# Moving the second FFN's row normalisation and quantisation into the attention batches of a two-layer kernel

## The reference

```python
x = x + _L1_xattn_ref(_layernorm(x), ctx_1024, ctx_1024, mask, Wq, bq, Wk, bk, Wv, bv, Wo, bo)
x = x + _L1_ffn_ref(_layernorm(x), gate_w, up_w, down_w, s_in, s_in_down)

def fake_quant_nvfp4(x, global_scale):       # blocks of 16 numbers
    amax = jnp.max(jnp.abs(xb), axis=-1, keepdims=True)
    sc8 = jnp.clip(amax / 6.0 * global_scale, 0.0, 448.0).astype(float8_e4m3fn).astype(float32)
    dq = sc8 / global_scale
    a = jnp.clip(jnp.abs(xb) / dq, 0.0, 6.0)
    return jnp.sign(xb) * nearest_of(0, 0.5, 1, 1.5, 2, 3, 4, 6)(a) * dq

def _L1_ffn_ref(x, ...):
    hidden = silu(fq(x) @ fq(gate_w).T) * (fq(x) @ fq(up_w).T)
    return fq(hidden) @ fq(down_w).T
```

## Time and profile before

| what | value |
|---|---|
| runs | 706.92 us median of three (706.83 to 707.96) |
| the profiled execution | 708.72 us, span 706.6 us |
| PE busy | 569.6 us (81% of the span) |
| DVE busy | 505.7 us (72%) |
| ACT busy | 377.0 us (53%) |
| POOL busy | 213.2 us (30%) |
| mean granted TensorE clock | 0.918 of full speed |
| chain that ended last | PE 42%, DVE 23%, ACT 13% of the span |

### The profile page before, as it was taken

One profiled execution on the slowest core, in us unless ns is written; L12 is line 12 of the kernel. 1 busy time (PEld: TensorE's weight loads), 2 busy tenths in 40 slices (PEclk: granted clock), 3 DMA queues, 4 the chain that ended last, 5 costly groups with the idle time before them and its releaser, 6 DMA issues.

```text
span 706.6 us, 14547 instructions
## 1 busy us (share of the span) xinstructions
PE 569.6 (81%) x4543; PEld 417.5 (59%) x4552; DVE 505.7 (72%) x1418; ACT 377.0 (53%) x717; POOL 213.2 (30%) x243
## 2 busy tenths in 40 slices
PE   5399999609999999976799999997535876687677
PEld 3188888509998898864466666664212453355345
DVE  6358887695655556573456666666769999999987
ACT  1324443113343333323666777778765878785674
POOL 5725774524665455552121443310000000000000
PEclk9789999959999999996899999999757999999999
DMA  8884443269466655607000000000000000000001
GB/s 317 271 221 132 129 150 119 71 217 387 148 220 200 204 180 179 207 28 241 1 2 0 0 0 0 0 1 2 4 1 0 31 15 16 31 30 16 16 30 60
DMA packets 35540, 68.49 MB, mean 97 GB/s; under 512 B 5581, under 2 KB 24542, under 8 KB 34464
## 3 DMA queue, kind: packets, MB, share of 16 engines
q1 hardware_dynamic: 28816, 52.37, 22.8%
q0 software_dynamic: 5520, 13.61, 5.6%
q10 hardware_dynamic: 1152, 1.88, 0.9%
HBM read 53.78 MB, written 15.80 MB: 98 GB/s over the span
## 4 chain that ended last, share of the span: by engine, by line
PE 42%; DVE 23%; ACT 13%; issue 8%; DMA 8%; SPq 4%; POOL 2%; DVEq 0%; POOLq 0%; ACTq 0%
PE quad L1128 10%; DVE hh L2234 5%; ACT nPT L874 4%; PE quad L1193 3%; PE bank L1264 3%; PE quad L1476 3%; DMA early<-in_W 3%; DMA x_after_ffn<-row,niU 2%; PE bank L1202 2%; ACT hqT L1022 2%; PE quad L1306 2%; PE quad L1283 2%; DVE nM L2081 2%; PE quad L1467 2%; DMA X<-x_after_ffn 2%
## 5 line engine op out<-in xcount | busy, mean ns | idle before, releaser
L777 ACT ACTIVATE hid<-quad,early 128x128 f32<-128x128 f32 x156 | 44.5, 368 | 83.8 <-PE quad L1193 83.8
L1193 PE MATMUL quad<-xts,early 128*128 128x128 f32 x624 | 74.9, 279 | 4.3 <-DMA early<-in_W 4.0
L1193 PEld LDWEIGHTS quad<-xts,early 128*128 128x128 f32 x624 | 73.2, 195 | 6.6 <-issue 5.0
L1202 PE MATMUL bank<-W2s,hid 128*128 x312 | 70.5, 379 | 0.0
L1202 PEld LDWEIGHTS bank<-W2s,hid 128*128 128x128 f32 x312 | 57.8, 190 | 7.1
L598 POOL DMA_INDIRECT x_after_ffn<-row,niU x39 | 38.9, 999 | 58.0 <-DVE row L1861 41.5
L1476 PE MATMUL quad<-uT,xqT 128*128 128x512 bf16 x128 | 40.1, 417 | 19.8 <-DVE hh L2234 18.9
L1856 DVE SCALAR_TENSOR_TENSOR row<-bank,sco,row 128x256 f32<-128x256 f32 x39 | 18.6, 476 | 46.1 <-PE bank L1202 45.7
L998 ACT ACTIVATE sil<-quad,gmx 128x512 f32<-128x512 f32 x64 | 41.0, 686 | 18.8 <-PE quad L1467 18.2
L2081 DVE TENSOR_REDUCE nM<-quad 128x32 f32<-128x2048 f32 x16 | 36.7, 2292 | 18.5 <-PE quad L1283 18.5
L564 POOL DMA_INDIRECT rows_by_expert<-row,pi x38 | 37.8, 996 | 33.8 <-DVE pi L1698 23.1
(11 more groups left out here) (365 smaller groups left out, 1325.0 us busy)
## 6 DMA issues: line engine op xcount, KB each, us to landing
early<-in_W SPq DMA_DIRECT2D x37, 514.0 KB, 5.5
row<-rows_by_expert SPq DMA_DIRECT2D x38, 134.0 KB, 2.2
early<-in_ctxO SPq DMA_DIRECT2D x4, 1024.0 KB, 8.0
ctxs<-in_ctxT SPq DMA_DIRECT2D x4, 1024.0 KB, 13.7
W2s<-in_W SPq DMA_DIRECT2D x8, 512.0 KB, 3.6
X<-x_after_ffn SPq DMA_DIRECT2D x7, 516.0 KB, 7.3
out<-yo SPq DMA_DIRECT2D x14, 256.0 KB, 2.1
early<-in_W ACTq DMA_DIRECT2D x2, 514.0 KB, 8.9
```

Of the source, the lines that this page charges most:

```text
L777: ins = act.activation(hid[:, u, c * P:(c + 1) * P], bank[2 + u][:, c * P:(c + 1) * P], ACT.Gelu, bias=W1r[:, k, DC * H2 + c:DC * H2 + c + 1])
L1193: ins = pe.matmul(bank[2 + u][:, n * P:(n + 1) * P], W1r[:, m % RING, c * H2 + n * P:c * H2 + (n + 1) * P], xt[:, u, c, :], start=c == 0, ...
L1202: ins = pe.matmul(bank[6 + u % 2][:, 0:D], hid[:, u, c * P:(c + 1) * P], W2s[:, bass.ds(ex, 1), c, :].rearrange("p o s -> p (o s)"), start ...
```

## The change

ACT no longer makes the bf16 copy in the same step as the absolute values: `rows_size` makes the one, `rows_half` the other, and each counts the semaphore `s_ax`, so that DVE waits for the first before the maxima and for the second before the scaling. The final scales are cut in parts of tiles 1 to 8, 9 to 16, and 17 to 32. Groups 0 and 1 pass all steps within attention, and group 2 up to its block maxima, each step given to one batch by its number; for that the batch loops of ACT, POOL and DVE are written out. Group 3 is normalised by ACT in the prologue, where DVE now finishes groups 2 and 3 with one scale computation. In the FFN's loop DVE's `group(g)` quantises rows g+3, for g from 1 to 4. ACT's `tile_norm(i + 4)` stays where it is in its group, and there are four `xq` buffers in the place of two. A second branch of the program for inputs with other bounds is changed likewise and doesn't run here.

```diff
-        done_parts = [slice(1, 9), slice(9, NTILE - 3), slice(NTILE - 3, NTILE + 1)]
+        done_parts = [slice(1, 9), slice(9, 17), slice(17, NTILE - 3), slice(NTILE - 3, NTILE + 1)]
...
-            def rows_normed(g, g0):
+            def rows_normed(g):
+                act.wait_ge(s_nm2, (4, 4, 5, 5, 6, 6, 6, 6)[g])
+                if g > 1:
+                    act.wait_ge(s_xq, g - 1)
...
-            def rows_halved(g, g0):
+            def rows_size(g):
                 act.wait_ge(s_x4, g + 1)
-                act.activation(absx[g0 % 2], top(x4s[g0 % 2]), ACT.Abs)
-                act.copy(xb[g0 % 2], top(x4s[g0 % 2])).then_inc(s_ax, 1)
-
-            def tile_norm(g, g0):
-                rows_normed(g, g0)
-                rows_halved(g, g0)
+                act.activation(absx[g % 2], top(x4s[g % 2]), ACT.Abs).then_inc(s_ax, 1)
+
+            def rows_half(g):
+                act.copy(xb[g % 2], top(x4s[g % 2])).then_inc(s_ax, 1)
...
                     exps(b)
-                    if stage == 1:
-                        done_roots(0)
-                    if stage == 2:
-                        act.wait_ge(s_nm2, 4)
-                        rows_normed(0, 0)
+                    if b in (5, 9):
+                        done_roots(b // 9)
...
                     if stage == 0:
                         rows_out(b + 2)
+                    if b in (6, 7, 12):
+                        rows_normed({6: 0, 7: 1, 12: 2}[b])
+                    if b in (7, 8, 13):
+                        rows_size({7: 0, 8: 1, 13: 2}[b])
                     if stage == 1:
                         weights_out(0)
                     inverse_sums(b)
+                    if b in (9, 10, 13):
+                        rows_half({9: 0, 10: 1, 13: 2}[b])
...
                     if stage == 2:
-                        rows_halved(0, 0)
-                        rows_normed(1, 1)
                         weights_out(4)
...
-                done_roots(1)
+                weights_out(5)
                 done_roots(2)
                 act.activation(tscr[:], tscr[:], ACT.Silu)
-                weights_out(5)
...
             x_out(0)
-            rows_halved(1, 1)
             for u in range(4):
                 silu(u, u, first=u < 2)
                 if u:
                     hidden_half(u - 1, u - 1)
+                if u == 1:
+                    rows_normed(3)
+                    rows_size(3)
+                    rows_half(3)
             hidden_half(3, 3)
-            act.wait_ge(s_nm2, 5)
-            tile_norm(2, 2)
-            act.wait_ge(s_xq, 2)
-            tile_norm(3, 3)
+            def tile_norm(g):
+                rows_normed(g)
+                rows_size(g)
+                rows_half(g)
...
                 if i + 4 < NGR:
-                    tile_norm(i + 4, i + 4)
+                    tile_norm(i + 4)
...
+            sized = [1, 2, 5, 7] + [2 * g + 1 for g in range(4, NTILE // 4)]
...
-            def rows_sizes(g, g0, steps):
-                v.wait_ge(s_ax, g + 1)
-                halves(absx[g0 % 2], halfx, 16, NBX // 16, big[:, rows_c], steps)
+            def rows_sizes(g, steps, c=rows_c):
+                v.wait_ge(s_ax, sized[g])
+                halves(absx[g % 2], halfx, 16, NBX // 16, big[:, c], steps)
...
+                def rows_between(b):
+                    if b == 6:
+                        done_scales(done_parts[0], 1, stn)
+                    if b == 8:
+                        rows_sizes(0, stn)
+                    if b == 9:
+                        done_stats(1)
+                        rows_sizes(1, stn, two_c[1])
+                    if b == 10:
+                        block_scales(both_c, stn)
+                    if b == 11:
+                        rows_quantised(0, stn)
+                    if b == 12:
+                        done_scales(done_parts[1], 2, stn)
+                        rows_scaled(1, stn, two_c[1])
+                        clamped(xf, stn)
+                    if b == 13:
+                        rows_rounded(1, stn, two_c[1])
+                    if b == 14:
+                        rows_sizes(2, stn)
...
                 if rows:
-                    rows_sizes(g + 2, g + 2, st)
+                    rows_sizes(g + 3, st)
                 hidden_sizes(g, st)
...
-            rows_sizes(1, 1, st)
-            product(0, 0)
-            product(1, 1)
-            block_scales(rows_c, st)
-            rows_scaled(1, st)
-            rows_quantised(1, st)
-            product(2, 2)
-            product(3, 3)
+            for u in range(4):
+                product(u, u)
+                if u == 1:
+                    rows_sizes(3, st, two_c[1])
+                    block_scales(both_c, st)
+            for g in (2, 3):
+                rows_quantised(g, st, two_c[g - 2])
             for g in range(NTILE // 4 - 1):
-                group(g, g + 2 < NTILE // 4)
+                group(g, 1 <= g and g + 3 < NTILE // 4)
```

More of the change, by code:

```diff
@@ L316, in two_layers_kernel @@
         nMT = sb("nMT", [P, S], BF16, en)
+        xqs = [sb(f"xq{k}", [P, 4, D], BF16, en) for k in range(1, 4)]
         en.close()
@@ L669, in _ @@
                 batch(5, 1, 3, k=1)
[L670 to L674, removed]
+                for b in range(6, NB - 2):
+                    batch(b, b % 2, b // 2 + 1, k=b - 4 if b - 4 < SLOTS else None)
             with pool.Else():
@@ L941, in _ @@
                 batch(6, 0, p=3, k=1)
[L942 to L945, removed]
+                for b in range(7, NB - 2):
+                    batch(b, b % 2, p=(b + 1) // 2, k=b - 5 if b - 5 < SLOTS else None)
                 batch(NB - 2, 0, p=NB // 2 - 1, stage=1)
                 batch(NB - 1, 1, stage=2)
-                done_roots(1)
+                weights_out(5)
                 done_roots(2)
                 act.activation(tscr[:], tscr[:], ACT.Silu)
-                weights_out(5)
             with act.Else():
@@ L976, in _ @@
                     weights_out(t)
[L977 to L982, removed]
+                for part in range(3):
+                    done_roots(part)
+                for g in range(2):
+                    rows_normed(g)
+                for g in range(2):
+                    rows_size(g)
+                for g in range(2):
+                    rows_half(g)
+                rows_normed(2)
+                rows_size(2)
+                rows_half(2)
                 act.activation(tscr[:], tscr[:], ACT.Silu)
@@ L1530, in _ @@
             pe.wait_ge(s_wTe, 6)
-            pe.wait_ge(s_dst, 3)
+            pe.wait_ge(s_dst, 4)
             x_in(1)
@@ L2139, in _, with scales_and_stats, between @@
                 batch(4)
-                batch(5, between=lambda: activation_scales(stn))
-                with v.Fori(0, SLOTS // 2) as i:
-                    stn.enter(i, 2 * (2 + 3))
-                    batch(i * 2 + 6, between=lambda: weight_rounded(i * 2, stn))
-                    batch(i * 2 + 7, between=lambda: weight_rounded(i * 2 + 1, stn))
-                    stn.leave(SLOTS // 2)
-                batch(NB - 2, between=lambda: done_stats(0))
-                done_scales(done_parts[0], 1, stn)
+                def scales_and_stats():
+                    activation_scales(stn)
+                    done_stats(0)
+                batch(5, between=scales_and_stats)
+                def rows_between(b):
[18 more added lines that the diff above has]
+                        rows_sizes(2, stn)
+                def between(b):
+                    if b - 6 < SLOTS:
+                        weight_rounded(b - 6, stn)
+                    rows_between(b)
+                for b in range(6, NB - 1):
+                    batch(b, between=lambda: between(b))
                 b = NB - 1
@@ L2208, in _ @@
                 stg.link(ins)
-                done_stats(0)
-                done_scales(done_parts[0], 1, stg)
-                done_stats(1)
-                rows_sizes(0, 0, stg)
-                block_scales(rows_c, stg)
-                rows_scaled(0, stg)
-                done_stats(2)
-                rows_quantised(0, stg)
+                for part in range(4):
+                    done_stats(part)
+                for part in range(2):
+                    done_scales(done_parts[part], part + 1, stg)
+                for g in range(2):
+                    rows_sizes(g, stg, two_c[g])
+                block_scales(both_c, stg)
+                for g in range(2):
+                    rows_quantised(g, stg, two_c[g])
+                rows_sizes(2, stg)
                 v.drain().then_inc(s_cdone, 1)
                 v.wait_ge(s_cdone, 3)
-            done_scales(slice(9, NTILE + 1), 3, st)
+            done_scales(slice(17, NTILE + 1), 3, st)
             ts(ones[:], ident[:], gmx[:, 5:6], gmx[:, 7:8], ALU.mult, ALU.mult)
```

47 lines of the change are left out of this document (27 added, 20 removed).

## The result

The changed kernel takes 735.23 us, the median of four runs (733.84 to 737.27); the kernel before took 707.44 us beside it (706.83 to 708.74, four runs). The ratio is 1.0393, with a 95% interval from 1.0358 to 1.0427: 3.9% slower. The medians lie 27.8 us apart. The profiled execution has a span of 732.1 us against 706.6, 25.5 us more.

What follows compares the result with a forecast made beforehand. DVE's in-order instruction list was taken to bound the FFN; +5.5 - 2.75 - 3.0 + 27.8 + 0.8 - 2.1 = +26.25 us, on a median of 706.92, gave 733.2 us, range 728 to 740.

Steps and rivals of the forecast that it cites:

- The loop: FFN groups 1 to 4: DVE waits 6.95 us at each head for ACT's late row copies, +27.8 us.
- The addition of 0.8 us for that clock: FFN groups 1 to 4: PE idles longer and runs at a lower clock, 0.2 us each, +0.8 us.
- ACT in attention: Attention batches 6 to 13: ACT row work beyond 1.0 us of room delays the next exponentials, +5.5 us in all.
- the idle 0.73 us: Attention: ACT's idle time before the queries' rows copy, taken not to hide row work standing behind it.
- the bound of 2.6: Attention: ACT's cost if the idle 0.73 us also hid work in four heavy batches; rival at 730.3 us, chance 0.17.
- DVE in attention: Attention batches 6 and 8 to 14: DVE's added row work all fits, 0; up to 0.6 if POOL interferes.
- the room of 2.49 us: Attention: DVE idle per batch, 1.82 us before adding the attention output plus 0.67 before the row maximum.
- The further 1 us: Attention batches 9 to 11: possible loss of a few tenths each by the DVE and POOL port lock, about 1 us.
- The seam: End of attention to group 0's transposed copy: earlier output add and roots, weight copy moved ahead, -2.75 us.
- The prologue and group 0: FFN start: ACT prepares group 3, DVE quantises groups 2 and 3, group 0 has no rows; -3.0 us.
- Groups 5 and 6: Late FFN loop: group 5 loses its rows, 21.61 instead of 23.72 us, -2.1; group 6 unchanged, 0.

Runs made afterwards that it cites:

- The first two experiments: Changed kernel with ACT's later normalisations one turn earlier: 707.55 us; changed kernel with them straight behind the last hidden copy, ahead of three copies: 722.83 us.
- the spread kernel: Against the first experiment: ACT's added attention work cut into pieces on both sides of the queries' rows copy, DVE's steps moved between batches; 699.89 us.
- the experiment with three repeats: Against the spread kernel: block maxima of group 0 computed three times instead of once on DVE in batch 8; the execution took 706.41 us.
- the first experiment: Against the changed kernel: ACT's normalisation of each later row group in the FFN loop made one turn earlier; 707.55 us.

## Why the prediction was right, step by step

The direction, the cause and the size were forecast, 733.2 us against 735.23. The change forecast was +26.25 us; without the layers ahead, which the edit does not touch, +27.3 was measured. The terms missed by 0.1 to 0.8 us each, with both signs, so part of the nearness of the sum is that misses cancel.

*The loop* was the step that carried it: four waits of 6.95 us were forecast from the earlier trace rows, 6.95, 6.99, 7.06 and 7.20 came. The growth is PE's: in the last, the second hidden copy out of a bank waited 0.19 us for transposes of PE that took 1.01 us, 0.61 where they were fast; the granted clock over these groups was 0.83, 0.93 before the change. The addition of 0.8 us for that clock was too high inside the groups: beyond the waits they lost 0.28. The waits grew by 0.4 that was not forecast, and the two misses nearly cancel. The first two experiments show the cause twice, by taking the waits away and by shortening them.

*ACT in attention*: +5.5 forecast, +5.19 measured, and by batch: +0.80, +1.69, +0.03, +0.29 and +0.33 in batches 6 to 10 (forecast 1.0, 2.0, 0, 0.35, 0.35), +1.03 and +0.97 in 12 and 13 (1.0, 0.8); batch 5, counted at nothing, took +0.22 (below), batch 11 gave 0.17 back, unexplained. That the idle 0.73 us ahead of the copy of rows doesn't help work that stands behind it was the choice against the bound of 2.6; the spread kernel, which puts work there, confirms it.

*DVE in attention* was put at 0 with up to 0.6 for one batch. No batch but the fifth shows more than ACT's part, so the value nearly held. In batch 5 ACT's new roots set its share of the weights 0.44 us later, and with it POOL's scaling of that share; DVE's steps that split the row maximum ran beside it and took 1.39 us from the end of the maximum in the place of 1.17, one of them 0.66 us instead of 0.19. And the room of 2.49 us was read too simply: an instruction of POOL's in it takes its time out of it. In batch 8 of the kernel after, DVE's maxima had ended when POOL's longer instructions began, and only the first halving was held (0.84 us); in the experiment with three repeats they had not. The Trainium skill, SBUF — State Buffer, section "SBUF: two separate sides", has a lock on the ports that VectorE and GpSimd share, by which the later of the two waits the whole instruction out. The halvings that lasted 1.43, 1.20 and 0.63 us, each until just behind the end of a POOL instruction, agree with it, and so does batch 14, where POOL is silent and nothing grew. The further 1 us that the prediction thought possible by it in batches 9 to 11 did not come: they took +0.29, +0.33 and -0.17, no more than ACT's part.

*The seam*: -2.75 forecast, -2.31 measured. The roots came 1.72 us sooner, better than the 1.45 forecast. PE's stop of 3.02 us ahead of the transposes wasn't foreseen; before the change PE waited 3.52 us for DVE at that place, so a stop of this length would not have shown. It cost ACT 0.65 us of idle where none was counted.

*The prologue and group 0*: -3.0 forecast, -2.16 measured. Timelines of DVE and PE after:

```profile
512.65 1.01 DVE L1947 TENSOR_TENSOR ctxs<-ctxs 128x512 bf16<-128x512 bf16 x3 [2.43 <-ACT ctxs L830]
...
516.54 1.89 PE L1481 MATMUL quad<-uT,xqT 128*128 128x512 bf16 x4 [1.16 <-DVE hh L2277]
517.68 1.60 DVE L2277 SCALAR_TENSOR_TENSOR hh<-quad,gmx,sil 128x512 f32<-128x512 f32 x2 [0.54 <-PE quad L1481]
...
523.90 0.95 DVE L1980 TENSOR_SCALAR ctxs<-wraw 128x3072 int16<-128x3072 int16 x1
```

ACT's absolute values came 10.1 us after the copy, as forecast (10.0), but the fourth tile's product waited 0.54 us for PE and took 1.60 us, 1.41 for the third, and group 0's hidden maxima began at 21.4 instead of 20.2. PE's four matmuls in front of that product took 1.89 us, 1.05 for such a set earlier in the prologue, and the granted clock over the prologue was 0.66: PE at its lower clock was counted in group 0 and forgotten here. Group 0 itself took 19.8 instead of 20.1.

*Groups 5 and 6*: -2.69 and +0.82 against -2.1 and 0. Both go with PE's clock in groups without rows (below). That they come within 0.2 us of the forecast together is luck: in the profiles of the experiments the two groups took from 40.12 to 43.94 us, 43.47 here.

## What to carry to other kernels

When a step is moved forward in one engine's list, the step that feeds it has to move by as many turns in the other engine's list: follow the producer back to what it waits for, and if that is the consumer's own last instruction, the whole list in between is paid in every turn. Idle time of an engine is room only where it stands: 2 to 3 us of row work in one block cost 0.8 to 1.7 us in a batch, the same work in pieces of 0.6 to 1.1 us on both sides of a wait cost nothing, and with the rows made a turn earlier the kernel came out about 1% faster than the one before. In these batches a room on VectorE reaches up to the next GpSimd instruction, not up to the next VectorE one.

## What the runs showed of the hardware beside this

Groups 5 and 6, where they quantise no rows, have the same work in every kernel, yet took 20.06, 20.93 to 21.61 or 22.35 to 22.53 us, and each length goes with a granted clock over it: 1.00, 0.92 and 0.85. Windows view of the spread kernel, groups 5 and 6:

```profile
635.61:655.67 20.06, 15.70 (x111) 9.44 (x112) 19.34 (x28) 14.70 (x19) 0.00 (x0) 1.00 0.08 27
655.67:678.02 22.35, 18.29 (x111) 11.10 (x112) 19.42 (x28) 14.74 (x19) 0.00 (x0) 0.85 0.07 25
```

PE's same 111 matmuls are busy for 2.6 us more in the second, DVE's busy time is the same within 0.1 us, and DVE has a wait for PE there that the first has not (timeline of DVE):

```profile
669.02 1.41 DVE L2285 SCALAR_TENSOR_TENSOR hh<-quad,gmx,sil 128x512 f32<-128x512 f32 x2 [2.20 <-PE quad L1491]
```

So up to 2.5 us of such a group go with the clock that PE is granted. A group with rows does not show it: in the first experiment group 4 took 23.72 us at a clock of 0.86, as group 1 did at 0.93, because DVE's own list sets its length. What in the work before decides between the three was not tried.
